# Routing by quarters of the experts, scores carried in the gathered rows, shared experts inside the expert loop, and the weight loads issued from ScalarE

## The reference, cut to what matters

```python
x = x + 0.5 * ffn(layernorm(x))
x = x + attention(layernorm(x))          # 16 heads, causal, not changed here
x = x + 0.5 * ffn(layernorm(x))

def ffn(x):                              # E = 64 experts, K = 6, CAP = 64, D = 128, I = 88
    scores = softmax(x @ gate_w.T)
    _, idx = top_k(scores + gate_b, 6)
    # per expert, in token order, only the first 64 tokens that chose it are kept
    h = silu(xb @ w1[e].T) * (xb @ w3[e].T);  yb = h @ w2[e].T
    y[token] += yb * scores[token, e]
    z = silu(x @ ws1.T) * (x @ ws3.T) @ ws2.T     # two shared experts, all tokens
    return y + z
```

## Time and profile before

| | |
|---|---|
| median of 3 runs | 580.01 us (578.88 to 585.59) |
| profiled execution | 577.09 us, of which its span is 575.3 us |
| mean granted TensorE clock | 0.741 |
| busy: PE, DVE, ACT, POOL | 416.0, 307.1, 242.1, 309.1 us |
| first pass, attention, second pass | about 0 to 223, 223 to 362, 362 to 575 us |

### The profile page before, as it was taken

The page is one execution under the profiler, slowest core; times in us unless marked ns, Lnnn a source line. Parts: engine busy times, 40 slices in busy tenths (PEclk is TensorE's granted clock), DMA queues, the critical chain, the costliest instruction groups (busy, mean ns, idle before and its releaser), DMA issues.

```text
span 575.3 us, 15281 instructions
## 1 busy us (share of the span) xinstructions
PE 416.0 (72%) x6016; PEld 272.2 (47%) x6016; DVE 307.1 (53%) x935; ACT 242.1 (42%) x637; POOL 309.1 (54%) x251
## 2 busy tenths in 40 slices
PE   0884765999479913488999996088586599857980
PEld 0842452555244512266887885084354255424450
DVE  6396991222110796344777664758999122212087
ACT  4972111333123348754767751298311133312330
POOL 7085777788888400303334430008978688888740
PEclk9978895555558965697999998558889555555896
DMA  8996900101002997000112112630000010100395
GB/s 266 394 263 256 347 14 8 8 5 12 6 7 69 400 408 292 1 3 0 38 39 50 44 50 48 226 146 2 0 1 11 7 9 6 9 7 5 101 405 224
DMA packets 34379, 60.25 MB, mean 105 GB/s; under 512 B 12611, under 2 KB 18846, under 8 KB 33870
## 3 DMA queue, kind: packets, MB, share of 16 engines
q1 hardware_dynamic: 23078, 58.41, 28.6%
q0 software_dynamic: 11264, 1.38, 2.7%
HBM read 37.43 MB, written 29.36 MB: 116 GB/s over the span
## 4 chain that ended last, share of the span: by engine, by line
PE 29%; DVE 26%; issue 16%; DMA 15%; POOL 7%; ACT 5%; SPq 1%; POOLq 0%; another core or an unknown queue 0%; DVEq 0%; ACTq 0%
DVE X L961 8%; DMA rows_d<-A 6%; PE upper L869 5%; POOL planes_d L437 4%; DMA planes_d<-Bb,put_i 4%; POOL A L451 4%; DVE Cb L1063 3%; ACT A L495 3%; PE bank L771 2%; DVE bn L966 2%; DMA Bb<-planes_d 2%; PE bank L826 2%; PE bank L885 2%; PE upper L903 2%; PE bank L854 2%
## 5 line engine op out<-in xcount | busy, mean ns | idle before, releaser
L437 POOL DMA_INDIRECT planes_d<-Bb,put_i x64 | 100.4, 1569 | 25.5 <-issue 20.1
L467 POOL TENSOR_TENSOR Bb<-Cb,chm 128x576 f32<-128x576 f32 x32 | 36.9, 1183 | 108.7 <-PE upper L914 69.0
L451 POOL DMA_INDIRECT A<-rows_d,tok_i x64 | 71.8, 1123 | 21.9 <-issue 17.1
L1093 DVE TENSOR_TENSOR ring<-ring,bank 128x88 f32<-128x88 f32 x64 | 15.7, 246 | 103.6 <-ACT ring L563 68.2
L668 PE MATMUL bank<-ident,A 128*128 128x128 f32 x96 | 21.7, 401 | 56.0 <-ACT A L495 39.1
L668 PEld LDWEIGHTS bank<-ident,A 128*128 128x128 f32 x96 | 17.3, 211 | 59.0 <-issue 32.6
L788 PE MATMUL upper<-w2s,ring 88*64 88x128 f32 x256 | 43.9, 446 | 0.0
L395 POOL TENSOR_TENSOR Bb<-Eb,st 128x512 f32<-128x512 f32 x8 | 8.9, 1113 | 62.0 <-DVE st L1011 62.0
L1097 DVE TENSOR_SCALAR Bb<-upper,sl 128x128 f32<-128x128 f32 x64 | 22.5, 351 | 32.0 <-PE upper L788 24.2
L771 PE MATMUL bank<-w1s,ring 128*64 128x88 f32 x256 | 35.5, 377 | 3.0 <-issue 1.9
L563 ACT ACTIVATE ring<-bank 128x88 f32<-128x88 f32 x64 | 15.5, 243 | 46.6 <-PE bank L771 30.3
(11 more groups left out here) (171 smaller groups left out, 1037.4 us busy)
## 6 DMA issues: line engine op xcount, KB each, us to landing
planes_d<-zeros SPq DMA_DIRECT2D x8, 2048.0 KB, 20.9
w3s<-in_w3T SPq DMA_DIRECT2D x2, 2816.0 KB
rows_d<-A SPq DMA_DIRECT2D x8, 512.0 KB, 11.0
A<-planes_d SPq DMA_DIRECT2D x8, 512.0 KB, 9.4
PL<-planes_d SPq DMA_DIRECT2D x8, 512.0 KB, 10.0
...
```

What stands on the lines that cost most here:

```text
L437: pool.indirect_dma_start(out=planes_d[f], in_=Y[:, s, :], in_offset=None, out_offset=bass.IndirectOffsetOnAxis(ap=put_i[:, s:s + 1], axis=0),
L451: pool.indirect_dma_start(out=A[:, t, :], out_offset=None, in_=rows_d, in_offset=bass.IndirectOffsetOnAxis(ap=tok_i[:, t:t + 1], axis=0), ...
L467: pool.tensor_tensor(out=VX[:, :, :, c, :].rearrange("p q h f -> p (q h) f"), in0=VN.rearrange("p q h f -> p (q h) f"), in1=chm[:, c:c + 1 ...
```

## The change

It moves work and replaces the method of routing; what is computed stays the same.

- Scores travel in the rows: `rows_d` has 192 columns, the 128 values and the 64 scores. SP writes both parts (the scores when POOL has made them), and a gather brings 192 values into a ring of 15 tiles, `GAT`. `weigh` takes its factor from there, in two instructions of 64 rows.
- Routing runs by quarters of 16 experts in bf16: `mask(h)`, `scan(h)` with a segment factor, `table(h)` with one comparison instead of two and a product, `differences(h)` on PE, `look_up(h)`, `slots(h)` for eight slot tiles. The counts no longer lie in `A`.
- The expert loop has no transpose back: `hidden` takes the weights as the stationary operand, so its output is already transposed.
- Two shared blocks (EARLY = 2) start beside the routing, the other six go through the expert loop, one part per tile (`shared_part`). POOL no longer takes part: products and additions stand on DVE.
- ACT, not SP, issues the loads of w1, w3, w2 and the zeros of the first pass's planes (`loads`), behind `normalise(2)` of the first norm.
- The four planes are interleaved by token, and 8 loads of 1024 KB take the place of 16 of 512 KB.

```diff
-    RW = 2 * NI + 1
-    PER = 7
-    NB = -(-NS // PER)
-    LEAD = (16, 6)
+    RC = NI + 1
+    RWD = D + NE
+    RING = 15
     NQT = 4
+    HE = NE // NQT
...
-                if f == 0:
-                    sp.wait_ge(zero_set, 1)
-                    clear_planes(0)
+                    sp.dma_start(rows_blk[:, GI * g:GI * g + GI, 0:D], A[:, GI * g:GI * g + GI, :]).then_inc(rows_out, 16)
+                for g in range(NG):
+                    sp.wait_ge(scores_ready, NG * f + g + 1)
+                    sp.dma_start(rows_blk[:, GI * g:GI * g + GI, D:RWD], SC[:, GI * g:GI * g + GI, :]).then_inc(scores_out, 16)
 
                 for k in range(2):
                     sp.wait_ge(added[k], 16 * (NS // 2) * (f + 1))
-                sp.wait_ge(z_added, NSH * f + EARLY)
+                sp.wait_ge(z_added, NSH * (f + 1))
...
+                    src = planes_d[f].rearrange("(p i k) d -> p i (k d)", p=P, k=4)
+                    dst = PLANES[g].rearrange("p (i w) -> p i w", i=GI)
+                    for h in range(2):
+                        half = slice(GI // 2 * h, GI // 2 * (h + 1))
+                        sp.dma_start(dst[:, half, :], src[:, GI * g + GI // 2 * h:GI * g + GI // 2 * (h + 1), :]).then_inc(part_in[g], 16)
                 if f == 0:
-                    clear_planes(1)
+                    clear_planes(sp, 1)
...
-                def counts():
-
-                    for h in range(NQT):
-                        ex = slice(HE * h, HE * h + HE)
-                        pool.wait_ge(base_ready, f + 1)
-                        pool.tensor_tensor(out=R[:, ex, 0:NI], in0=CUM[:, ex, :],
-                                           in1=st2[:, 4, ex].unsqueeze(2).broadcast_to([P, HE, NI]),
-                                           op=ALU.add).then_inc(counts_ready, 1)
...
-                    ahead = min(NS, s + 1 + max(LEAD[1], LEAD[0] - s // 2))
+                    ahead = min(NS, s + RING)
...
-                        pool.indirect_dma_start(out=A[:, t, :], out_offset=None, in_=rows_d,
+                        pool.indirect_dma_start(out=GAT[:, t % RING, :], out_offset=None, in_=rows_d,
...
-                for g in range(EARLY, NSH):
-                    shared_gates(g)
...
+                def loads():
+                    act.wait_ge(zero_set, 1)
+                    for dst, src in ((w1s, w1T), (w3s, w3T), (w2s, w2T)):
+                        act.dma_start(dst[:, :, :], src).then_inc(w_in, 16)
+                    clear_planes(act, 0)
...
                         normalise(j - 1)
+                        if n == 0 and j == 3:
+                            loads()
...
+                for n in range(2 * EARLY):
+                    act.wait_ge(sh_ps, 2 * f * NSH + n + 1)
+                    a, b3 = EARLY_BANKS[n % 2]
+                    act.activation(SHE[n], bank[a][0:I, :], ACT.Silu)
+                    act.activation(H3E[n], bank[b3][0:I, :], ACT.Copy).then_inc(sh_silu, 1)
+
+                act.wait_ge(rows_out, 16 * NG * (f + 1))
+                act.activation(DR[:, :, NI], c32[:, 0:1].broadcast_to([P, NE]), ACT.Copy)
+                for h in range(NQT):
+                    act.wait_ge(dr_ps, NQT * f + h + 1)
+                    act.activation(DR[:, HE * h:HE * h + HE, 0:NI], bank[3 + h % 2][:, :].rearrange("p (e i) -> p e i", e=HE),
+                                   ACT.Copy).then_inc(dr_sb, 1)
+
+                def shared_silu(g, k):
+                    n = (f * NSH + g) * 2 + k
+                    act.wait_ge(sh_ps, n + 1)
+                    act.wait_ge(sh_gated, n - 1)
+                    act.activation(SH[k], bank[SHARED[0]][0:I, :], ACT.Silu).then_inc(sh_silu, 1)
 
                 def copy_xbT(s):
...
-                                shared_out(EARLY - 3 + s // PER)
-
+                def differences(h):
+                    ex = slice(HE * h, HE * h + HE)
+                    pe.wait_ge(scanned, NQT * f + h + 1)
+                    pe.matmul(bank[7][:, HE * h:HE * h + HE], before_b[:, :], CUM[:, ex, NI - 1], start=True, stop=True).then_inc(lo_ps, 1)
+                    if h >= 2:
+                        pe.wait_ge(dr_sb, NQT * f + h - 1)
+                    bk = bank[3 + h % 2][:, :].rearrange("p (e i) -> p e i", e=HE)
+                    pe.matmul(bk, step_b[:, :], CUM[:, ex, :], start=True, stop=False)
+                    pe.matmul(bk, next_b[:, :], CUM[:, ex, NI - 1:NI].broadcast_to([P, HE, NI]), start=False, stop=True).then_inc(dr_ps, 1)
+
+                def look_up(h):
+                    pe.wait_ge(table_ready, NQT * f + h + 1)
+                    pe.wait_ge(dr_sb, NQT * f + h + 1)
+                    if h >= 2:
+                        pe.wait_ge(tokens_ready, NQT * f + h - 1)
+                    for j in range(HE):
+                        k, q = j % 2, j // 2
+                        ins = pe.matmul(bank[LOOK[h % 2]][CAP * k:CAP * k + CAP, q * RC:(q + 1) * RC],
+                                        G[:, h, :, j], DR[:, HE * h + j, :], start=True, stop=True)
+                    ins.then_inc(look_ps, 1)
 
                 for g in range(EARLY):
...
+                    for k in range(2):
+                        shared_hidden(g, k)
+                pe.wait_ge(sh_silu, 2 * (f * NSH + EARLY))
+                pe.wait_ge(cast_done, 1)
+                for h in range(NQT):
+                    differences(h)
+                    look_up(h)
                 pe.wait_ge(w_in, 48 + 16 * f)
...
                     if s >= 2:
                         pe.wait_ge(gated, f * NS + s - 1)
-                    for w, off in ((w1s, 0), (w3s, I)):
+                    for w, off in ((w1s, 0), (w3s, P)):
                         for k in range(2):
-                            ins = pe.matmul(bank[2 + s % 2][CAP * k:CAP * k + CAP, off:off + I], XBT[s % 2][:, CAP * k:CAP * k + CAP],
-                                            w[:, 2 * s + k, :], start=True, stop=True)
+                            cols = slice(off + CAP * k, off + CAP * k + CAP)
+                            ins = pe.matmul(bank[2 + s % 2][0:I, cols], w[:, 2 * s + k, :],
+                                            XBT[s % 2][:, CAP * k:CAP * k + CAP], start=True, stop=True)
...
-                    if 2 <= s <= NS + 1:
-                        g_turn(s - 2)
-                    if s >= 3:
-                        expert_out(s - 3)
-
-                for g in range(EARLY, NSH):
-                    for k in range(2):
-                        shared_hidden(g, k)
-                    if g > EARLY:
-                        shared_out(g - 1)
-                shared_out(NSH - 1)
+                    if s >= 2:
+                        expert_out(s - 2)
+                    part = shared_part(s)
+                    if part and part[1] < 2:
+                        shared_hidden(*part)
+                    elif part:
+                        shared_out(part[0])
...
+                    for k in range(4):
+                        then(dve.tensor_tensor(xt, xt, PLANES[g].rearrange("p (i k d) -> p i k d", i=GI, k=4)[:, :, k, :], ALU.add))
...
+                def mask(h):
                     ex = slice(HE * h, HE * h + HE)
...
+                    return dve.tensor_tensor(M[:, ex, :].rearrange("p e i -> p i e"), RP[:, :, ex], BI[:, :, ex], ALU.not_equal)
+
+                def scan(h):
+                    ex = slice(HE * h, HE * h + HE)
+                    dve.tensor_tensor_scan(CUM[:, ex, :].rearrange("p e i -> p (e i)"), seg[:, :],
+                                           M[:, ex, :].rearrange("p e i -> p (e i)"), 0.0, ALU.mult, ALU.add)\
+                        .then_inc(scanned, 1)
+
+                def table(h):
+                    ex = slice(HE * h, HE * h + HE)
+                    dve.wait_ge(lo_ps, NQT * f + h + 1)
+                    then(dve.tensor_scalar(lo_b[:, ex], bank[7][:, ex], float(CAP), None, ALU.min))
+                    dve.tensor_tensor(G[:, h, :, :], slot_ce[:, :, ex], lo_b[:, ex].unsqueeze(1).broadcast_to([P, CAP, HE]),
+                                      ALU.is_ge).then_inc(table_ready, 1)
...
+                    then(dve.tensor_scalar(LE[:, 0:QSL, :], bk[:, :, 0:NI], c_of_p[:, 0:1], None, ALU.is_le))
+                    then(dve.tensor_reduce(sl[:, 0, ss], LE[:, 0:QSL, :], AX, ALU.add))
+                    then(dve.tensor_tensor(sl[:, 1, ss], sl[:, 0, ss], bk[:, :, NI], ALU.add))
...
+                    dve.scalar_tensor_tensor(put_i[:, ss], sl[:, 1, ss], 4.0, plane0[:, ss], ALU.mult, ALU.add)\
+                        .then_inc(tokens_ready, 1)
+
+                then(mask(0))
+                scan(0)
+                then(mask(1))
+                table(0)
+                scan(1)
+                then(mask(2))
+                slots(0)
...
+                    dve.wait_ge(z_ps, f * NSH + g - 1)
+                    dve.tensor_tensor(HSL[g % 2][k], SH[k], bank[SHARED[1]][0:I, :], ALU.mult).then_inc(sh_gated, 1)
+
+                def shared_add(g):
```

(9 more changed lines are left out.)

344 lines of the change are left out of this document (131 added, 213 removed).

## The result

The changed kernel takes 599.64 us in the median of 4 runs (599.05 to 599.80), the kernel before 582.80 (578.88 to 587.33): a ratio of 1.028, with a 95% interval of 1.0195 to 1.037, whose lower end is just under 2%. Measured once more as a control of the experiments it took 598.81 against 582.41 us, a ratio of 1.029 (1.025 to 1.034). So it is slower, by 2.8 to 2.9%. The forecast was 580 us, no change; 599.64 lies in the range of 546 to 604, at the place of the rival "PE becomes the bound of the loop", half low, which was priced at 594.

What follows compares the result with a forecast made beforehand. POOL's own work was taken to fill the expert loop's 110.0 us, with DVE's routing ahead of it; 577.1 + 45.5 - 19.5 - 17.7 - 4 - 4.5 = 576.9, with the median 2.9 above the profiled execution: 580 us, range 546 to 604.

Steps and rivals of the forecast that it cites:

- PE becomes the bound of the loop: Rival, expert loops: clock half low, +7 us per pass, 594 (chance 0.17); low throughout, +28, 636 (above 604: 0.10).
- ACT's stall, to the first mask: First pass: issuing weights and fills holds ACT, so copies to `XT` start at 66 instead of 20.5 us: +45.5.
- routing, first and second pass: DVE, mask to first gather: 10.3 us instead of 29.8 in the first pass, 9.2 instead of 26.9 in the second.
- expert loops: First gather to loads of the planes, POOL as the bound: 108 us instead of 110.0, -2 per pass.
- the rest: sums of planes, norms, attention: Outside routing and loops only the sums of the planes were forecast to change: -4.5 us over both passes.
- ACT does not stall: First rival, first pass: ACT's issues are short, mask stays at 43.2 us; time 534 to 555, chance 0.18.
- three quarter masks at 4.34 / 4 = 1.1 us: Routing on DVE: each quarter mask takes a quarter of the whole mask's 4.34 us, 3.3 us for three.
- 84 us, well below 105: Expert loop: PE's turns and shared blocks, high clock from the sixth turn, sum to 84 us against POOL's 104.7.
- the 2 us for all of POOL's waits: Expert loop, each pass: 2 us allowed for POOL's waits on earlier scatters, within the 108 us.
- POOL's own 104.7: Expert loop, each pass: 32 gathers and 32 scatters, 21.8 + 23.1 + 59.8 = 104.7 us.
- the clock rose as chosen: Expert loop: shared products in 12 of 32 turns bring PE's high clock from the sixth turn on; low throughout, 131 us.
- The sum of the planes: Behind the loops: without shared blocks' POOL products DVE's additions are no longer slowed, -1.8 and -2.8 us.

Runs made afterwards that it cites:

- x1: Changed kernel with the four zero fills of the first planes issued by SP behind the score stores instead of by ACT, weights staying on ACT: 561.53 us.
- x4: Changed kernel with the quarter masks written as f32 in two alternating buffers instead of as bf16: 583.81 us.
- x3: Changed kernel with the shared experts of the six later groups left out on PE, ACT and DVE: 591.49 us.
- x5: Changed kernel with the last shared group's three parts moved from turns 26 to 28 to behind the last turn of the expert loop: 590.31 us.

## Why the prediction was wrong

Against the span of before, forecast and measured, now with the routing counted from the first mask to the first gather, as the forecast did:

| term | forecast | measured |
|---|---|---|
| ACT's stall, to the first mask | +45.5 | +43.3 |
| routing, first and second pass | -19.5, -17.7 | -17.0, -14.2 |
| expert loops | -2, -2 | +7.4, +6.4 |
| the rest: sums of planes, norms, attention | -4.5 | -4.4 |
| sum | -0.2 | +21.5 |

**The stall** was right in mechanism, place and nearly in size, though its price came from another engine's queue. `x1` shows it alone. That the first gather of the first pass came at 99.2, where the forecast had 99, is luck: up to the first score product it was 3.3 us less than forecast, from there to the gather 3.5 us more. With the stall goes the first rival, "ACT does not stall" (534 to 554): it was the design's idea. Moving the fills to SP brings 561.5, above that range because the loops are slower than the forecast had them. The sentence of the Trainium skill that was weighed there ("DMA: Bandwidth & Descriptors", section "Issuing engines are not separate DMA queues": issuing time is "usually small relative to the DMA itself") holds in this trace for ACT's first four issues, 0.4 to 0.7 us, and not for the three behind them, 43.7 us together.

**The routing** was 6 us too good, a wrong size. The step that failed is "three quarter masks at 4.34 / 4 = 1.1 us": three masks of 2.37 us are 3.9 us more per pass. The cause is the type of the result, not the shape (`x4`). The scans (1.22 against 1.3) and the table (0.86 with its bound against 1.0) came out a little shorter, the slots and the hidden work on PE and ACT as put, and the casts of the first pass stand ahead of its first mask and not behind it (0.9 us), so the misses counted from the mask are 2.5 and 3.5 us. I had divided a duration of an f32 result and not asked what else the change did to that instruction.

**The loop** is the step that turned the sign, 17.8 us in the two passes. The step that failed is the comparison "84 us, well below 105", PE's sum against POOL's sum, and with it the 2 us for all of POOL's waits. In the second pass they are 10.8 us above the usual: 3.1 before the first scatter, 3.8 at the half clock behind it, 3.9 at the end. With POOL's own 104.7 and the 1.2 until the loads that is 116.7, and 116.4 was measured. PE's turns were sized well enough (11.0 us for four at the high clock, against 4 x 1.35 + 5.1 = 10.5; PE busy 92 in all, against 84), the clock rose as chosen, and in the middle POOL is the bound as said. But POOL's need per turn falls from 3.23 to 1.87 us when the gathers run out, and PE's stays at 2.75 while shared parts are left. `x3` and `x5` show it: 4.7 us per pass with all the later shared work out, 1.9 for one group moved. The rival had PE as the bound, and +7 for a half-low clock. That this is what the loops measured is partly luck: half of what PE cost came in the last turns, at the high clock, where the rival did not look. The first turns cost the rest. I had the first scatter follow the 15 gathers at 21.8 us; it came at 24.1, and 1.5 to 3 us of every pass there are pauses that neutral edits shorten and whose cause is open. At half clock the two early shared outputs (3.75 us, where I had put 3.0) and the first products of the next group then held POOL for 3.8 us; `x3` keeps the outputs, 2.4 of these, and has loops of 111 to 112 us, not 108.

**The sum of the planes** came at -3.3 us in the second pass (-2.8 forecast); DVE's additions take 1.25 us each, as forecast.
